# Softmax denominators of two head pairs in one group of matmuls, a new table of slots, and a last norm whose additions two engines share

## What is computed

```
h = layernorm(x) * (1 + ca) + sa
q = h @ Wq.T;  latent = h @ Wkv_down.T;  k, v = latent @ Wk_up.T, latent @ Wv_up.T
attn = softmax(q @ k.T / 8) per head                # 16 sequences x 8 heads, 512 x 512 each
x = x + ga * (attn @ v) @ Wo.T
h = layernorm(x) * (1 + cb) + sb
y = moe(h) + h                                      # top 2 of 8 experts, capacity limited
x = x + gb * (layernorm(y) * gamma + beta)          # the last norm, over all 8192 tokens
```

## Time and profile before

| | us |
|---|---|
| median of 3 runs (lowest, highest) | 1332.85 (1331.63, 1333.52) |
| the profiled execution, its own time | 1331.5 |
| span of its profile, first to last instruction | 1329.8 |

### The profile page before, as it was taken

The page is one execution under the profiler, slowest core; times in us unless marked ns, Lnnn a source line. Parts: engine busy times, 40 slices in busy tenths (PEclk is TensorE's granted clock), DMA queues, the critical chain, the costliest instruction groups (busy, mean ns, idle before and its releaser), DMA issues. The chain is left out here.

```text
span 1329.8 us, 23668 instructions
## 1 busy us (share of the span) xinstructions
PE 1153.5 (87%) x5959; PEld 770.8 (58%) x5960; DVE 975.3 (73%) x2248; ACT 748.2 (56%) x1454; POOL 936.3 (70%) x1075
## 2 busy tenths in 40 slices
PE   7899999999999999999999999999987127889800
PEld 5556566666666565666666665656554025889800
DVE  4888686777777776777777777867675897567676
ACT  4566656576566656665655666566642431344436
POOL 4586969687878869697878779697865203546438
PEclk9899999999999999999999999999998555899955
DMA  4000101010101101010101010010102412314196
GB/s 155 16 20 17 48 18 49 17 64 1 64 16 48 48 16 48 16 62 2 64 1 64 16 48 33 17 33 17 49 1 79 113 63 67 61 33 111 27 304 205
DMA packets 68478, 70.91 MB, mean 53 GB/s; under 512 B 12912, under 2 KB 64032, under 8 KB 68272
## 3 DMA queue, kind: packets, MB, share of 16 engines
q1 hardware_dynamic: 46800, 47.18, 11.0%
q10 hardware_dynamic: 16896, 16.78, 3.8%
q0 software_dynamic: 4704, 6.11, 2.9%
HBM read 40.35 MB, written 29.45 MB: 52 GB/s over the span
## 5 line engine op out<-in xcount | busy, mean ns | idle before, releaser
L717 ACT ACTIVATE PF<-PS 128x512 f32<-128x512 f32 x512 | 298.4, 595 | 256.7 <-PE PS L1124 248.5
L1016 DVE TENSOR_REDUCE NMAX<-PS 128x1 f32<-128x512 f32 x512 | 342.6, 682 | 88.5 <-PE PS L1133 84.8
L579 POOL TENSOR_TENSOR SF<-SF,PF 128x512 f32<-128x512 f32 x252 | 323.2, 1304 | 14.0 <-ACT PF L717 13.8
L1205 PE MATMUL PS<-PF,V 128*64 128x512 f32 x1024 | 248.0, 605 | 0.0
L1123 PE MATMUL PS<-Q,K 128*128 128x512 f32 x512 | 221.9, 433 | 2.6 <-ACT PF L717 2.5
L1133 PE MATMUL PS<-K,Q 128*128 128x512 f32 x512 | 205.8, 404 | 11.0 <-DVE NMAX L1016 10.9
L1124 PE MATMUL PS<-Q,K 128*128 128x512 f32 x512 | 201.5, 394 | 0.0
L736 ACT ACTIVATE Q<-PS 64x512 fp32r<-64x512 f32 x256 | 151.7, 593 | 48.2 <-PE PS L172 43.3
L656 POOL TENSOR_TENSOR XL<-XF,XH 128x512 fp32r<-128x512 f32 x63 | 82.9, 1316 | 131.1 <-ACT XH L794 131.1
L576 POOL TENSOR_TENSOR SF<-PF 128x512 f32<-128x512 f32 x126 | 162.4, 1305 | 5.8 <-ACT PF L717 5.3
L1123 PEld LDWEIGHTS PS<-Q,K 128*128 128x128 f32 x512 | 96.4, 188 | 120.0 <-issue 55.2
(11 more groups left out here) (361 smaller groups left out, 2427.2 us busy)
## 6 DMA issues: line engine op xcount, KB each, us to landing
X<-in_L_attn_x SPq DMA_DIRECT2D x16, 512.0 KB, 3.3
MODB<-mod_rows SPq DMA_DIRECT2D x16, 512.0 KB, 3.6
h_rows<-H ACTq DMA_DIRECT2D x16, 512.0 KB, 3.0
acc_rows<-H ACTq DMA_DIRECT2D x16, 512.0 KB, 4.1
out_x<-X SPq DMA_DIRECT2D x16, 512.0 KB, 2.9
A<-acc_rows SPq DMA_DIRECT2D x15, 512.0 KB, 8.9
W1F<-in_L_ffn_W SPq DMA_DIRECT2D x3, 1024.0 KB
W2F<-in_L_ffn_W SPq DMA_DIRECT2D x3, 1024.0 KB
```

The source lines that it names most:

```text
L579: s_sum.done(pool.tensor_tensor(total, total, tile, ALU.add))
L717: s_exp.done(act.activation(PF[:, u % 8, :], st_bank(u), ACT.Exp))
L1016: s_mred.done(dve.tensor_reduce(NMAX[:, p % 2, r:r + 1], mx_bank(u), AX.X, ALU.max, negate=True))
L1205: last = pe.matmul(num_bank(p)[odd * R:(odd + 1) * R, :], V1[:, vp, c, :], PF[:, k % 8, :], start=(c == 0), stop=(c == TC - 1))
```

## The change

It touches two places.

**Attention.** (a) "den" is now one job for two pairs: four matmuls with 32 columns of ones, one for each head, each writing its own 32 partitions of one bank. A batch has two such groups, den 0 in slot 18 and den 1 in slot 36 (slot 4 of the next body), where it had four of two matmuls, in slots 12, 20, 28 and 36. (b) VectorE transposes such a bank once, takes eight reciprocals of 32x16 that also spread each head over 64 partitions, and then transposes back and multiplies once for each pair. (c) Since the even pair's numerators must leave their PSUM bank before the division, ScalarE copies them into a new tile NUMS, which VectorE then multiplies. (d) The table gets other numbers nearly everywhere. The last batch keeps the old form for its pairs 2 and 3.

**The last norm.** (e) The chain of the first group is written in one go in the first six slots of the next group's statistics. (f) Every fourth pair (q % 4 == 3) is multiplied in place in PSUM and added to X by VectorE; GpSimd adds the other 24.

```diff
-    AHEAD, PV_AT, ADD_LAG, DIV_AT, XH_AT, NORM_AT, MOD_AT, OUT_AT = 13, 4, 2, 12, 16, 19, 41, 63
-    STAT_AT, XN1_AT, XN2_AT, H2_AT, GBB_AT = (2, 6, 6, 9), (2, 2, 4, 5), (50, 51, 52, 53), (52, 55, 57, 59), (58, 62, 71, 72)
-    AT = {("mrow", 1): 4, ("mrow", 2): 12, ("mrow", 3): 20, ("mrow", 0): -4, ("den", 0): 12, ("den", 1): 20, ("den", 2): 28,
...
+    AHEAD, PV_AT, ADD_LAG, NORM_AT, MOD_AT, OUT_AT = 14, 4, 2, 19, 42, 67
+    XH_AT, FINAL_XH, FINAL_DEN, KEEP_AT = (22, 27, 39, 40), (23, 25, 32, 40), {2: 28, 3: 36}, (19, 26)
+    STAT_AT, XN1_AT, XN2_AT, H2_AT, GBB_AT = (0, 9, 12, 13), (3, 3, 4, 4), (48, 50, 51, 56), (52, 53, 56, 57), (53, 53, 70, 71)
+    AT = {("mrow", 1): 4, ("mrow", 2): 11, ("mrow", 3): 20, ("mrow", 0): -5, ("den", 0): 18, ("den", 1): 36, ("q", 0): -18,
...
                 if c == 1:
-                    s_den.wait(pool, b, p - 2)
+                    s_den.wait(pool, b, p // 2 - 1)
...
+                    for g, tb in due(KEEP_AT, b, n):
+                        if not (final(tb) and g):
+                            s_pv.wait(act, tb, 2 * TC * g + TC - 1)
+                            s_xlo.wait(act, tb - 1 + g, 2 - 2 * g)
+                            s_kept.done(act.activation(NUMS[:, :], num_bank(2 * g), ACT.Copy))
...
+            def normalise_group(xb, g, part, place):
+                base = GROUP_OPS * g
                 if (part, place) == (0, 1):
+                    s_den.wait(dve, xb, g)
...
+                    s_x.done(dve.transpose(XF[:, :], job_bank(DENS[g])))
+                elif (part, place) == (1, 0):
+                    s_x.wait(dve, xb, base)
+                    for i in range(2):
+                        for k in range(4):
+                            head = slice((2 * i + k // 2) * 32, (2 * i + k // 2 + 1) * 32)
+                            s_x.done(dve.reciprocal(RDEN[k * 32:(k + 1) * 32, i, :], denominators(XF[head, :])))
+                elif (part, place) in ((1, 1), (2, 1)):
+                    s_x.wait(dve, xb, base + BACK[part - 1] - 1)
+                    s_x.done(back(XF[:, :], RDEN[:, part - 1, :]))
+                elif (part, place) == (2, 0):
+                    s_x.wait(dve, xb, base + BACK[0])
+                    s_kept.wait(dve, xb, g)
+                    s_x.done(dve.tensor_tensor(NUMS[:, :], NUMS[:, :], XF[:, :], ALU.mult))
+                elif (part, place) == (3, 0):
...
+                    s_x.done(dve.tensor_tensor(XF[:, :], num_bank(1), XF[:, :], ALU.mult))
...
+                        if kind == "den" and exists(b + off) and not (final(b + off) and g):
+                            wait_job_bank(pe, b, job)
+                            s_sum.wait(pe, b + off, 4 * (TC - 1) * (g + 1) - 1)
+                            for head in range(4):
+                                last = pe.matmul(job_bank(job)[head * 32:(head + 1) * 32, :], ONE[:, 0:32], SF[:, head // 2, head % 2, :],
+                                                 start=True, stop=True)
+                            s_den.done(last)
...
+            if by_vector(q):
+                dve.tensor_tensor(normalised, normalised, gain, ALU.mult).then_inc(s_vadd, 1)
+                dve.wait_ge(s_vadd, 2 * (q // 4) + 1)
+                x = X1[:, 2 * q:2 * q + 2, :]
+                dve.tensor_tensor(x, normalised, x, ALU.add).then_inc(s_vadd, 1)
+            else:
+                dve.tensor_tensor(A[:, 2 * q:2 * q + 2, :], normalised, gain, ALU.mult).then_inc(s_mul, 1)
```

159 lines of the change are left out of this document (102 added, 57 removed).

## The result

| | us |
|---|---|
| changed kernel, median of 6 runs (lowest, highest) | 1342.24 (1339.35, 1346.49) |
| kernel before, beside it | 1333.36 (1331.63, 1334.34) |
| ratio | 1.0073, 95% interval 1.0060 to 1.0086 |
| span of the profile, changed and before | 1340.0 and 1329.8 |

The change makes the kernel slower by 0.73%; the forecast was 1.6% faster. It was wrong in its direction.

What follows compares the result with a forecast made beforehand. TensorE's full queue was taken to bound attention. Savings of 15 x 1.28 + 0.5 = 19.7 us there and 1.0 in the last norm, 20.7 in all, took the median 1332.85 to 1312 us, range 1303 to 1326.

Steps and rivals of the forecast that it cites:

- Zero, with 0.3 us either way: Attention: projections, norms and transposes moved to other slots add no instruction, so cost nothing, give or take 0.3 us.
- fifteen batches with both groups as equal: Attention: fifteen batches each have both denominator groups and each gain 1.28 us on TensorE.
- Four tiles abreast, the group's cost, TensorE's gain: Attention denominators: four column tiles run at once, 0.86 us a group, so TensorE gains 1.28 us a batch.
- The rivals with a price for the tiles or by twos: Denominators: a group costs 1.08 us (1319 us, chance 0.08), or 1.72 by twos (1338.7 us, 0.09).
- VectorE's burst: Behind den 0: VectorE needs 7.35 to 7.95 us, TensorE 7.2, so TensorE waits 0.5 us in slot 23.
- so both cancel: Attention: the new 0.5 us wait behind den 0 replaces the old 0.48 us a batch, net nothing.
- the third rival: Behind den 0: NUMS product waits for a whole GpSimd addition, slot 23 wait 1.6 us; 1328.5 us, chance 0.09.
- GpSimd as a hard second limit: Between den 0 and den 1: GpSimd 25.6 us, TensorE 25.4, only just not late; wait up to 0.3 us possible.
- which gives 0.86 - 0.34 = 0.5: Last batch: it has only one joined group, so TensorE gains 0.5 us there.
- wrong in its 1.0 us: Last norm: GpSimd's additions fall from 30 to 24 us, but only 1.0 us comes out, VectorE and ScalarE standing behind.
- Its rival on the slow side: Attention denominators: four tiles of 32 columns go by twos, a group costs 1.72 us; 1338.7 us, chance 0.09.

Runs made afterwards that it cites:

- e6: Changed kernel with two reciprocals of 128 x 16 instead of eight of 32 x 16 per group, leaving out the head-to-partition mapping: 1329.07 us, ratio 0.9979.
- e5: Changed kernel with the next batch's jobs (queries, latents, transposes, first maxima row, look-ahead 13) in their old slots: 1375.70 us, ratio 1.0325.
- e4: Changed kernel with the attention output of a batch back in slot 63 instead of 67: 1337.99 us, ratio 1.0049.
- e10: e12 with GpSimd's X + MODB additions of the second norm (GBB_AT) in slots 58, 62, 71, 72 instead of 53, 53, 70, 71: 1326.43 us, ratio 0.9958.
- e9: Changed kernel with the second norm, its transposes, the router's product and their bank times in the old slots: 1435.55 us, ratio 1.0774.
- e3: Changed kernel with the old timetable's numbers for everything but the joined denominators and what belongs to them: 1451.53 us, ratio 1.0900.
- e12: Changed kernel with den 0's second transpose back and odd pair's product two slots later, and the output in slot 63: 1328.60 us, ratio 0.9972.

## Why the prediction was wrong

Of the 31 us between the forecast's span and the measured one 5.7 lie in batches 2 to 12 and 25 outside of them. By the table those are 5.2 up to the first scores, 4.4 in batches 0 and 1, 6.3 in batches 13 and 14, 5.3 in the last batch, 3.2 from there to the last norm, and 1.0 in it. Two steps failed above all: the prediction put the moved jobs at "Zero, with 0.3 us either way", wherever in the program they stand, and it counted fifteen batches with both groups as equal.

- **Four tiles abreast, the group's cost, TensorE's gain: right.** 1.06 us and 1.00 to the next scores (forecast 1.05 and 0.95). Of the gain of 1.28 us a batch 1.15 come out where VectorE doesn't hold it up (e6). The rivals with a price for the tiles or by twos fell.
- **VectorE's burst: right in mechanism and slot, mis-sized.** Forecast 0.5 us in slot 23, "so both cancel"; it is 0.75 by the waits and 1.0 by the slot, which is what counts. The reciprocals (0.245) were right. The NUMS product came out at 1.16 us on average for 1.1, but by luck, since it is two cases: 0.73 to 0.98 behind den 0, where it counts, and 0.69 to 1.87 behind den 1, where nobody waits for it (1.68 or more in five of eight). In 15 of these 16 cases it ends 0.55 us after a GpSimd instruction does, so in the long cases a whole addition ran first, as the third rival had it, only not behind den 0. Missing were the 0.3 us until VectorE starts, and the drain that the recorded waits hide. The period, 59.97 for 59.4, is mostly this term; the 0.57 us would be 8.5 over 15 batches.
- **GpSimd as a hard second limit: right that it isn't.** TensorE's denominators wait for it 0.0 us.
- **The moved jobs at "Zero, with 0.3 us either way": the step that failed first.** The forecast priced them with the cover that they have in the loop. Ahead of the first scores there is no such cover, and the same numbers cost 4.5 us from the first L170 (e5, with the old slots of the next batch's jobs, takes all of it back). Batches 0 and 1 lose 1.8 more where 2.6 should have been gained; that part has no experiment of its own.
- **Fifteen batches treated as equal: the second.** Two of them are written out behind the loop, and there the output moved to slot 3 costs 4.4 us (e4; 3.2 by the ratios). It makes GpSimd late, then TensorE wait for XL, and then the granted clock falls to 0.50. That the stop itself is instruction fetch fits and is not shown.
- **The last batch, "which gives 0.86 - 0.34 = 0.5": the third.** It costs 4.8 in the profiled execution, since the additions of GBB_AT (L692) stand ahead of the H product that TensorE waits for (3.8 us), and the granted clock falls behind that wait. e10 takes back 2.2 us by the medians. The prediction had neither this wait nor any term for a clock that falls after one.
- **The last norm: right in its chain, wrong in its 1.0 us.** The chain ends 3.5 us later counted from the first statistics (forecast 2.9), ScalarE takes 12.1 us more as forecast, and GpSimd is still last, 0.3 us behind VectorE, where the forecast had it 0.4 ahead. Most of the 1.0 us that was to come out is in these two terms, 0.6 in the chain and 0.3 at GpSimd:

```profile
1321.78 0.17 DVE L2082 SCALAR_TENSOR_TENSOR NMR<-PS,Yr 128x16 f32<-128x16 f32 x1
...
1326.04 8.04 ACT L2143 ACTIVATE PS<-A,NMR,Yr 128x256 f32<-128x256 f32 x16
...
1332.16 3.71 POOL L2151 TENSOR_TENSOR X<-X,A 128x512 f32<-128x512 f32 x3 [0.32 <-DVE A L2096]
```

- **Its rival on the slow side was the wrong one.** It came near the measured time (1338.7 for 1342.2) by another road, for the four tiles do not go by twos. It asked of the tiles what it should have asked of the table: what do these numbers do where the loop isn't in its steady state?

**Open.** The 1.9 us between the last score and the last router product and the 0.9 us behind them: with the old second norm (e9) and the old table (e3) the first is 0.8, the second was 0.0 in e6 alone. For the first the clock is a part: its mean over that stretch is 0.79 before, 0.82 in e9 and 0.72 in the changed kernel, and TensorE is busy 0.8 us longer. For the second I have no cause. Nor is it shown what still holds GpSimd for 2.5 us behind the loop in e4, what holds ScalarE in the first body behind it, or what TensorE waits for in its 2.12 us at the start.

## What to carry to other kernels

A table that sets the order of a pipelined loop also sets its start, its tail and any body written out behind it; cost a new table on each of these apart, since work that is hidden in the loop stands bare there. Where a burst on one engine ends just as another needs it, an estimate that comes out even was a wait of 1 us a batch here; moving two operations past the point of need gave 0.64 of it back, and removing six 0.87. A table fits one set of jobs: parts of it, put back, cost 1.6 to 7.6 us a batch, while the slots of the output and of GBB cost the loop nothing. And a wait of 3 us can cost TensorE more than its length, since twice the clock fell behind one: look at the granted clock behind each long wait.

## What the hardware showed that I had not expected

- Four fp32 matmuls of 32 columns and 512 values on four column groups take 1.06 us together, as two of 64 did (1.03 in the earlier trace rows).
- A reciprocal of 32 x 16 takes 245 ns, one of 128 x 16 takes 224 (e6). A quarter of the partitions saved nothing, so eight small ones cost 2.2 us.
- TensorE's granted clock was 0.50 right after waits of 3.1 us (slot 11 of batch 14) and 3.2 us (last batch of e12), and stayed at 1.00 after one of 1.6 (e4).
- With all 16 DMA engines at 0.80 busy for 4 us by one 1 MB output, GpSimd started an addition 3.8 us late in a body written out behind the loop; with the output 4 slots earlier, 2.5 us. The releaser that the profile named had been done for over 6 us.
